# Gathering every tile of node features on GpSimd in a graph-attention layer

## The reference

```python
h = jnp.maximum(_layernorm(x, axis=-1), 0.0)                 # (12500, 64)
h_edge = ((h[src] + bond) @ W).reshape(-1, H, D)             # one row of h per edge
h_node = (h @ W).reshape(-1, H, D)
el = jnp.einsum('ehd,hd->eh', h_edge, attn_l)
er = jnp.einsum('nhd,hd->nh', h_node, attn_r)
s = el + er[dst]
s = jnp.where(s > 0, s, 0.2 * s)
alpha = softmax of s over the edges that share a dst
ft = segment_sum(h_edge * alpha[..., None], dst).mean(axis=1)
out = x + relu(batch_norm(ft) * bn_gamma + bn_beta)
```

## Time and profile before

| | |
|---|---|
| median of 3 runs | 3058.62 us (3056.72 to 3063.78) |
| span of the profiled execution | 1885.4 us |
| median less span | 1173.2 us |
| POOL busy | 1389.6 us, 74% |
| DVE busy | 1312.1 us, 70% |
| PE busy | 1042.3 us, 55% |
| ACT busy | 1041.5 us, 55% |
| gathers by POOL | 1467 |

### The profile page before, as it was taken

The page is one execution under the profiler, slowest core; times in us unless marked ns, Lnnn a source line. Parts: engine busy times, 40 slices in busy tenths (PEclk is TensorE's granted clock), DMA queues, the critical chain, the costliest instruction groups (busy, mean ns, idle before and its releaser), DMA issues.

```text
span 1885.4 us, 47594 instructions
## 1 busy us (share of the span) xinstructions
PE 1042.3 (55%) x6860; PEld 792.2 (42%) x6860; DVE 1312.1 (70%) x4737; ACT 1041.5 (55%) x8591; POOL 1389.6 (74%) x1477
## 2 busy tenths in 40 slices
PE   2726646556545744655554565545654654564466
PEld 1614534444434533533443353434433543453355
DVE  7878877776676766776766866766766667667676
ACT  2520366666655665666565565665665565566522
POOL 7777677777777777777777777777777777777770
PEclk9857766667666766666666666666666666676667
DMA  8643232232222223222322232232223222222335
GB/s 232 172 107 96 61 89 72 64 95 66 64 84 77 64 64 97 64 64 63 98 64 64 63 98 64 63 97 64 64 63 98 64 63 79 82 64 63 97 72 140
DMA packets 77196, 156.31 MB, mean 83 GB/s; under 512 B 34116, under 2 KB 38736, under 8 KB 70224
## 3 DMA queue, kind: packets, MB, share of 16 engines
q1 hardware_dynamic: 28818, 99.91, 15.9%
q0 software_dynamic: 46944, 49.57, 13.1%
q10 hardware_dynamic: 1112, 3.73, 0.8%
HBM read 141.85 MB, written 9.80 MB: 80 GB/s over the span
## 4 chain that ended last, share of the span: by engine, by line
POOL 59%; issue 21%; PE 7%; DVE 7%; DMA 2%; ACT 2%; ACTq 1%; DVEq 0%; SPq 0%
POOL work L698 58%; PE po L1084 2%; ACT cols L840 1%; PE p_s L985 1%; ACTq L468 1%; PE p_s L947 1%; DMA er_run<-er_tab,er_idx 1%; DMA acc<-in_x 1%; PE pt L972 1%; DMA h_tab<-acc 1%; PE p_s L1014 1%; PE pt L936 1%; DVE work L1215 0%; DVE onehot L1358 0%; POOL er_run L712 0%
## 5 line engine op out<-in xcount | busy, mean ns | idle before, releaser
L698 POOL DMA_INDIRECT work<-h_tab,srcI x1396 | 1319.7, 945 | 430.0 <-issue 423.5
L840 ACT ACTIVATE cols<-acc 32x2 f32 x8352 | 928.3, 201 | 493.8 <-issue 460.6
L1084 PE MATMUL po<-scaled,work 128*65 128x64 f32 x3104 | 297.4, 284 | 60.5 <-issue 57.5
L1084 PEld LDWEIGHTS po<-scaled,work 128*65 128x65 f32 x3104 | 292.0, 200 | 78.0 <-issue 77.1
L1466 DVE COPY cols<-acc 32x2 f32 x1376 | 178.1, 189 | 160.6 <-issue 142.0
L972 PE MATMUL pt<-ident,work 128*128 128x128 f32 x784 | 194.7, 391 | 59.4 <-DVE work L1215 59.3
L1022 PE MATMUL p_s<-ident,elh 128*32 128x128 f32 x196 | 50.6, 411 | 303.9 <-DVE elh L1210 303.9
L1210 DVE COPY elh<-work 128x16 f32<-128x16 f32 (+2 forms) x222 | 40.5, 195 | 227.0 <-DMA work<-h_tab,srcI 225.1
L1570 DVE TENSOR_TENSOR acc<-acc,po 65x64 f32 x776 | 168.4, 217 | 28.0 <-PE po L1084 1.6
L985 PE MATMUL p_s<-work,wpair 128*32 128x256 f32 x784 | 180.5, 384 | 1.6 <-DVEq L1165 1.6
L972 PEld LDWEIGHTS pt<-ident,work 128*128 128x128 f32 x784 | 139.0, 200 | 88.6 <-DVE work L1215 64.2
(11 more groups left out here) (219 smaller groups left out, 1271.0 us busy)
## 6 DMA issues: line engine op xcount, KB each, us to landing
row_tile<-h_tab SPq DMA_DIRECT2D x3392, 0.3 KB
work<-in_ea_t SPq DMA_DIRECT2D x49, 1024.0 KB
ohT_i<-in_dst_n SPq DMA_DIRECT2D x49, 512.0 KB
work<-h_tab,srcI POOLq DMA_INDIRECT x1396
acc<-hT_tab SPq DMA_DIRECT2D x2, 1562.5 KB, 14.4
h_tab<-acc SPq DMA_DIRECT2D x1, 2887.5 KB
work<-in_x SPq DMA_DIRECT2D x1, 2800.0 KB
out<-work SPq DMA_DIRECT2D x5, 448.0 KB
```

Source lines behind the costliest of these rows:

```text
L698: pool.indirect_dma_start(out=row, out_offset=None, in_=x if c < RAW else h_tab, in_offset=bass.IndirectOffsetOnAxis(ap=srcI[:, c, j, g:g ...
L840: copied = nc.scalar.activation(view(cols[0:HALF, n % COL_BUFS, 0, i:i + 1], [[P, H]]), view(acc[CP:P, 0, bass.ds(r, 1)], [[NACC, H]]), AC ...
L1084: m = mm(bank[0:F1, w0:w0 + H * WIN], edge[c % 2][:, j, g, :], scaled[:, j * CG + g, :, :].rearrange("p h w -> p (h w)"), start=(j == 0), ...
```

## The change

`ROW_FIRST` goes from 6 to `NCH - 1` = 48 and `COL_FIRST` from 5 to `NCH` = 49. So `col_tiles(c)` is empty for all chunks, and `row_tiles(c)` for all but the last, which keeps its tile of 64 edges. `tiles_of` gives the 76 + 26 = 102 tiles to POOL. The waits for column copies, which now have none to wait for, are taken out.

```diff
@@ -50,12 +50,12 @@
 ROW_BUFS = 4
-ROW_FIRST = 6
+ROW_FIRST = NCH - 1
...
 COL_G = 12
-COL_FIRST = 5
+COL_FIRST = NCH
@@ -600,8 +600,6 @@
-            sp.wait_ge(cols_ok, col_batches_upto(NCH - 1)[0])
-            sp.wait_ge(cols_dve_ok, col_batches_upto(NCH - 1)[1])
             sp.wait_ge(zT_ok, Z_IN)
@@ -844,7 +842,6 @@
                 if c == NCH - 1:
-                    act.wait_ge(cols_dve_ok, col_batches_upto(c)[1])
                     z_keep(NZ - 5, zT_made, zT_ok)
```

## The result

The changed kernel took 2373.75 us (median; 2367.31 to 2391.95), beside 3060.08 us for the kernel before: a ratio of 0.7776, with a 95% interval of 0.7742 to 0.7811. I had forecast 3184.4 us, slower, with a range of 3174 to 3270. The direction was wrong.

The account below looks back on a forecast made before the run. The prediction took POOL's gathers, 1.25 us each, as the bound. It summed +127.5 - 0.8 - 0.9 = +125.8 us onto the median, 3058.6 + 125.8 = 3184.4 us, with a range of 3174 to 3270.

Parts of the forecast that it names:

- What bounds the kernel: Whole kernel: bound by the number of gathers on POOL times 1.25 us, until the last begins at 1842.56 us.
- My forecast keeps it as it is: Outside the traced span: the 1173.2 us by which the median exceeds it stay unchanged.
- the 9 to 15 us: Around the kernel: the Trainium skill's figure for preamble and postamble, taken to support a fixed part but not its size.
- +102 gathers: POOL's queue: 102 more gathers at 1.25 us each add 127.5 us.
- Nobody on the path waits for SP. Zero: SP's queue: removing 3328 of 3392 row DMAs and the register loads between saves nothing.
- beside POOL's gathers: ACT's 8352 and DVE's 1376 column copies: they run alongside POOL, so removing them saves only 0.8 us.
- The wait at 278 us: POOL's 1.08 us wait for PE's turned exponentials of chunk 5, behind ACT's column copies: goes, -0.8 us.
- the end: After the last gather: cover of 0.97 us means chunk 48's extra gather is not all paid; -0.9 us taken with the wait.
- Rival 1: Time outside the span grows with gathers, 0.80 us each, +81.6 us: 3266.0 us; chance 0.13.
- Rival 2: Time outside the span falls with the instruction count, 48% fewer, -563 us: about 2620 us; chance 0.07.
- Rival 3: POOL's gathers get cheaper without DVE's column copies; 0.08 us less each would give a level 3059 us; chance 0.02.
- Rival 4: POOL's wait at place 17 for the previous chunk's exponentials shows; 1 us over cover gives +43 us, 3227 us; chance 0.04.

Follow-up runs that it names:

- e14: Changed kernel with `ROW_FIRST` back at 6, so only the 76 column tiles go to POOL: 2809.95 us with stepping, 0.9205 of the kernel before.
- e16: Kernel before with `ROW_FIRST` at `NCH - 1`, so only the 26 single-row tiles go to POOL: 2998.97 us with stepping, 0.9828 of the kernel before.
- e6: Kernel before with two column tiles in every chunk but the last and a second copy batch on DVE, 11 gathers fewer: 1888.76 us calm, ratio 1.0013.
- e15: Kernel before with a single-row tile in every chunk from 6 on, 16 gathers fewer: 3790.84 us with stepping, 1.2421 of the kernel before.

## Why the prediction was wrong, point by point

- **What bounds the kernel: right for the trace, wrong for the times.** POOL at 1.25 us per gather bound the traced execution. It did not bind the executions that gave 3058.62 us, and I had a number that said so: 1173.2 us of time without an instruction. I treated a gap of 62% as a remainder to carry along, though with such a gap a trace may not be of the timed thing at all.
- **"My forecast keeps it as it is": this is the step that failed.** The forecast carried 1173.2 us outside the span through the change as a constant. There is no such part, nor the 9 to 15 us that the prediction set beside it: span and time differ by under 3 us in every execution that has both, 1.74 us in the changed kernel's, and 3047.9 for 3049.57 us in one of the kernel before with stepping. The 1173 us were inside: late instruction starts, in queues that the change empties. Of them the changed kernel keeps 363 (2373.75 beside 2010.98).
- **+102 gathers: right.** +127.5 us was the term; calm, the whole change measured +123.4 us against a sum of +125.8, and the halves +89.7 for 76 and +29.1 for 26, so 1.12 to 1.21 us per gather net of what else the changes save.
- **"Nobody on the path waits for SP. Zero", "beside POOL's gathers" for ACT: right when calm, and the costliest miss.** I named no price for a lost cover on SP. It could be read from the trace: 31.7 us of row DMAs and three loads in a chunk of 36 to 37 us. ACT's could be read too: from 212.5 to 1807.8 us its column copies were busy for 928.3 us and their issue took 460.6, so 1389 of 1595 us were taken. At 0.68 us a DMA on the mean instead of 0.40 SP's cover is gone, and the rows cost 2809.95 - 2373.75 = 436 us with the columns out; the columns, with the rows out, cost 2998.97 - 2373.75 = 625 us.
- **The wait at 278 us and the end:** -0.8 and -0.9 us were too small to tell apart; the calm span came out at 2010.4 for 2011.2. (The landing that I took as 2.44 us is 2.46 by the rows named, 405.01 to 407.47; it changes nothing.)
- **Rival 1 (the outside goes with the gathers): fallen.** The changed kernel has more gathers and lost most of that time.
- **Rival 2 (it goes with the number of instructions): the right side, for a reason that is partly right.** It gave 2620 us, the measured time is 2374. A count alone is refuted by e14 and e16: removing 20986 of 47594 records (columns) gave 240 us, removing 7040 more (rows) gave 436. What counts is whose queue the instructions stand in and who waits behind them. I gave it 0.07, and its time lay outside of my range.
- **Rival 3: no gather got cheaper** (944 to 946 ns in the traces with stepping and without). **Rival 4** did show itself, in the stepping trace (37.6 us of waits for p_m by name) and in e6, by delays that I had excluded.

**What stays open.** What makes the engines step. By trace, or by time and clock where there is no trace, it was there in every execution on two of the seven chips of the experiments and in none on the five others (2823.41 us apart, which fits neither); six of them were met once, so it can't be said whether it belongs to the chip or to the time. It falls beside runs of gathers, which the calm traces have too. The starts lie on one raster for PE and DVE (changed kernel), for ACT and DVE (e16), and for PE and SP (e14: 482.51 and 482.48 us). The times of single instructions on DVE, ACT and POOL stay as they are, as a rule (DVE's L1361 takes 1.21 us at 1169.77 in the changed kernel's trace, 1.22 on the mean before), and so does the time between gathers that wait for nothing. PE's products are at one of the two times that they have when calm, but more often at the longer: the median for L982 (L985 before) is 379 ns before and 631 in e14, where the granted clock was 0.625 and not 0.66. The queues' own instructions do grow: the register instruction before a row DMA takes 29 to 38 ns when calm and up to 1407 ns in e14, so it isn't the DMAs alone that are slow. That the chain of the kernel before lies on SP and ACT with stepping is argued from e14, e15 and e16, not seen in a trace of it.

## What to carry to other kernels

Before any sum, set the traced execution's span beside the timed median: where they differ by more than a few per cent, the bound in the trace need not be the bound in the time, and a forecast needs a branch for each. Work that is moved off the slowest engine in hundreds of small instructions is free only while its queue is shorter than the bound; state that queue's length per round (here 33 of 36 to 37 us on SP) and what happens when it is one and a half times as long. When two such queues run side by side, an experiment on one of them shows little, and only taking both out shows what they cost. Where an engine is slow only at times, look at what the others do just then: a mean of 0.68 us per row DMA hides that it goes with the gathers.

## What the runs showed of the hardware that I had not expected

- On two of seven chips, in all executions there, instruction starts fall on a raster of 0.70 us in stretches of some 10 to 25 us, on several engines at once, while DVE's, ACT's and POOL's instructions themselves last as long as ever, as a rule. The same program then takes 3050 to 3060 us instead of 1888 (1.62 times), the changed one 2374 instead of 2011 (1.18 times). No row shows what causes it.
- The stretches lie beside gathers of POOL that follow one another without a pause, and end 2 to 7 us after the last has started: ACT made 15 copies in 15 us beside gathers and 83 in 13 us of a pause (e16).
- SP issued a single-row DMA per 0.40 us (80 in 31.73 us) and per 0.67 to 0.69 us in such an execution (80 in 53.28 and 55.36).
- Gathers on POOL that waited for nothing were 1.25 us apart on the mean in every trace read, with stepping and without (944 to 946 ns and some 0.31 us between). The Trainium skill ("SBUF — State Buffer", on the two sides of SBUF) would have a float32 copy on VectorE from SBUF to SBUF block a gather's descriptors; with 1376 column copies on DVE and with none of them, a gather took 944 to 945 ns, so the traces show no such effect for these copies of 32 x 2 elements.
